# A four-layer kernel on one core: tile steps, group ends and tail of the first layer rearranged

## The reference, cut to what matters

```python
xBC = silu(causal_conv(xBC, conv_w))           # width 4, per channel
dt = softplus(dt_raw + dt_bias); a = dt * -exp(A_log)
cum = cumsum(a) within a chunk of 128 tokens
Yd   = (C B^T * exp(cum_i - cum_j) * dt_j, lower triangle) @ xs
S    = S * exp(cum_last) + states of the chunk;  Yoff = exp(cum) * C @ S_before
y = (Yd + Yoff + D * xs) * silu(z)
yn = y * rsqrt(mean(y * y) + eps) * norm_w;    x += yn @ W_out.T
...
x += shared expert + sum over the 2 chosen experts of share * (silu(g) * u) @ w_down[e]
```

```python
qkv = xn @ w_qkv.T + b;  out = softmax(q k^T / 16) v @ w_out.T
scale = max(mean(|w|), 1e-8);  w = clip(round(w / scale), -1, 1)   # for w1 and w2
```

## Time and profile before

| | |
|---|---|
| three runs | 1669.63, 1669.21, 1664.41 us; median 1669.21 |
| the profiled execution | 1666.6 us, span 1664.9 us, mean granted clock 0.895 |
| PE busy | 1332.4 us (80%), 7251 instructions |
| DVE, ACT, POOL busy | 914.0 (55%), 535.9 (32%), 409.2 (25%) |
| DMA | 88.83 MB, mean 53 GB/s |

### The profile page before, as it was taken

One profiled execution on the slowest core, in us unless ns is written; L12 is line 12 of the kernel. 1 busy time (PEld: TensorE's weight loads), 2 busy tenths in 40 slices (PEclk: granted clock), 3 DMA queues, 4 the chain that ended last, 5 costly groups with the idle time before them and its releaser, 6 DMA issues. The chain is left out here.

```text
span 1664.9 us, 21457 instructions
## 1 busy us (share of the span) xinstructions
PE 1332.4 (80%) x7251; PEld 823.5 (49%) x7251; DVE 914.0 (55%) x1888; ACT 535.9 (32%) x885; POOL 409.2 (25%) x380
## 2 busy tenths in 40 slices
PE   5556787779777675799999987998655599988987
PEld 3334544554455344457766744544343264644564
DVE  4755455536553766512211378988867435557434
ACT  1444336623752362221212222332302122233321
POOL 3267214512443365200040011000013500000035
PEclk9776999999999877899999988999855698999999
DMA  9122112210222122300000060000001200111113
GB/s 356 51 85 92 36 29 74 80 28 27 94 63 60 37 98 72 113 0 1 0 0 0 0 228 0 0 1 0 1 3 38 83 19 20 32 39 57 55 48 114
DMA packets 68240, 88.83 MB, mean 53 GB/s; under 512 B 15334, under 2 KB 51494, under 8 KB 67497
## 3 DMA queue, kind: packets, MB, share of 16 engines
q1 hardware_dynamic: 61996, 70.76, 12.9%
q0 software_dynamic: 6144, 16.79, 3.3%
HBM read 61.14 MB, written 26.38 MB: 53 GB/s over the span
## 5 line engine op out<-in xcount | busy, mean ns | idle before, releaser
L387 PE MATMUL l_banks<-l_xnT,all_region_a 128*128 128x512 f32 x288 | 131.5, 612 | 0.0
L1819 PE MATMUL l_banks<-l_xnT,mid_region_c 128*128 128x512 f32 (+1 forms) x192 | 96.2, 654 | 17.5 <-DVE l_xnT L2002 17.5
L853 POOL TENSOR_TENSOR all_region_b<-all_region_b,l_lc 128x512 f32<-128x512 f32 x64 | 84.8, 1344 | 83.2 <-DMA all_region_b<-l_lc_rows 83.1
L2662 POOL TENSOR_TENSOR l_rstd<-l_moments,all_neg_half 128x4 f32<-128x4 f32 x20 | 20.6, 1030 | 337.5 <-DVE l_moments L2702 337.5
L867 POOL TENSOR_TENSOR l_rw<-l_xdt,l_decay 128x512 f32<-128x512 f32 x64 | 69.9, 1120 | 76.0 <-DVE l_xdt L1104 76.0
L387 PEld LDWEIGHTS l_banks<-l_xnT,all_region_a 128*128 128x128 f32 x288 | 56.0, 197 | 65.2 <-issue 63.7
L387 PE MATMUL l_banks<-all_region_a,l_xa 128*128 x234 | 68.8, 414 | 20.6 <-issue 14.1
L1124 DVE TENSOR_TENSOR all_region_b<-all_region_b,l_cbd 128x512 f32<-128x512 f32 x64 | 65.7, 1028 | 19.4 <-ACT all_region_b L696 15.4
L1819 PEld LDWEIGHTS l_banks<-l_xnT,mid_region_c 128*128 128x128 f32 (+1 forms) x192 | 37.7, 202 | 68.3 <-issue 49.5
L696 ACT ACTIVATE all_region_b<-all_region_b 128x512 f32<-128x512 f32 x64 | 69.2, 1081 | 4.3
L1077 DVE SCALAR_TENSOR_TENSOR l_xbc<-l_pre,all_cols,l_xbc 128x512 f32<-128x512 f32 x72 | 61.6, 856 | 5.8 <-issue 0.4
(11 more groups left out here) (442 smaller groups left out, 2860.9 us busy)
## 6 DMA issues: line engine op xcount, KB each, us to landing
all_region_b<-l_lc_rows SPq DMA_DIRECT2D x64, 256.0 KB
l_xa<-slots_in SPq DMA_DIRECT2D x39, 128.0 KB, 3.2
slots_out<-l_xa SPq DMA_DIRECT2D x39, 128.0 KB, 3.3
mid_vector_rows<-slots_in SPq DMA_DIRECT2D x39, 128.0 KB, 2.1
slots_out<-all_region_a SPq DMA_DIRECT2D x39, 128.0 KB, 1.7
slots_in<-l_xp SPq DMA_DIRECT2D x4, 1024.0 KB, 12.7
all_region_a<-l_gate_up SPq DMA_DIRECT2D x1, 4096.0 KB, 14.4
all_x<-x SPq DMA_DIRECT2D x4, 512.0 KB, 6.0
```

The costliest lines, as they stand in the source:

```text
L387: return nc.tensor.matmul(out, lhsT, rhs, start=start, stop=stop, **kw)
L853: nc.gpsimd.tensor_tensor(bc[:, k, :, :], bc[:, k, :, :], spread(lc[:, c, heads], 1, BLK), ALU.subtract).then_inc(dd_ready.sem, 1)
L1819: return nc.tensor.matmul(out, lhsT, rhs, start=start, stop=stop)
L2662: nc.gpsimd.tensor_tensor(rstd[:, :], moments[:, :, 1], mem.neg_half[:, 0:GT], ALU.pow).then_inc(rstd_ready.sem, 1)
```

## The change

- Tile steps start at group 0's chunk 3; six of group 1's and 2's places are doubled in their stead. Within a step the order becomes transposes of f, gate/up of f-1, down of f-3, transpose of f-2, on PE and in the bank table; ACT copies the transposes first. The expert's number for the next gate/up product is read behind the present one (`owner_of`).
- `from_before` is cut: the far product (`within_chunk`) is made behind the first near product. DVE's `from_state` is cut too (`next_state`); in chunk 0 it stands before the first near product.
- Group ends: the first projection of the next group and the sums (now in banks 4 to 6) come before the last output product; DVE and ACT follow, with `out_stats` and `out_add` of the last chunk behind convolutions 0 and 1.
- Head: five of group 0's convolutions lie between the transposed copies of the head.
- POOL: all scatters of the first 8 tiles before group 0's differences, the other 8 tiles two at a time within chunks 0 and 1; all fetches have places of their own, 12 tiles are fetched before group 3's first weights; the adds lie four per chunk in group 3.
- Layer 1's folds, ternary weights, first statistics and first normalisation are done in layer 0's last group and behind it. Shared places in SBUF change so that these live on (`mem.xa`).

```diff
@@ places, bank order
-    places = [... if (g, c) >= (0, 2)]
-    places = sorted(places + [places[-1], places[-3]])
+    places = [... if (g, c) >= (0, 3)]
+    places = sorted(places + [places[4 * i + 6] for i in range(STEPS - len(places))])
-        back = (("gu", f - 1), ("th", f - 2), ("dn", f - 3), ("tx", f))
+        back = (("tx", f), ("gu", f - 1), ("dn", f - 3), ("th", f - 2))
+        names.insert(len(names) - (CONV_BLK + Z_BLK - 1 if g > 0 else 0), ("sums", g))
@@ PE
+        def owner_of(i):
+            if i < MOE_TILES:
+                expert[i] = pe.value_load(owner[0:1, i:i + 1], min_val=0, max_val=N_EXP - 1)
         def tile_step(f):
...
-                n = expert[i] = pe.value_load(owner[0:1, i:i + 1], min_val=0, max_val=N_EXP - 1)
...
                 jobs.fill(last, ("gu", i))
+                owner_of(i + 1)
...
         for g in range(GROUPS):
-            sums(g)
             if g > 0:
...
-                for j in range(CONV_BLK + Z_BLK):
+                in_proj(g, 0)
+            sums(g)
+            if g > 0:
+                out_proj(g - 1, NCH - 1)
+                for j in range(1, CONV_BLK + Z_BLK):
                     in_proj(g, j)
...
                     near(g, c, k)
+                    if k == 0:
+                        within_chunk(g, c)
...
+                if (g, c) == (GROUPS - 1, 2):
+                    pe.wait_ge(weight_sum, 1)
+                    jobs.wait_room(pe, 0, "weight_mean")
+                    jobs.fill(mm(jobs.bank("weight_mean")[:, 0:2], ones[:, :], wabs[:, :]), "weight_mean")
                 assemble(g, c)
-            out_proj(g, NCH - 1)
+        pe.wait_ge(l1.fold_sem, 16 * 2)
+        fold("w_qk", 0, l1.qkv[:, DK:2 * DK, :])
+        fold("w_vo", 2 * DK, l1.out)
+        out_proj(GROUPS - 1, NCH - 1)
+        fold_biases()
@@ ACT
+            if g > 0:
+                in_proj(g, 0)
+                square(g - 1, NCH - 1)
             block_sums(g)
...
+                if (g, c) == (GROUPS - 1, 1):
+                    act.wait_ge(l1.sem, 16 * 2)
+                    for i, part in enumerate((l1.w1, l1.w2)):
+                        last = nc.scalar.activation(below, part.rearrange("p a n -> p (a n)"), ACT.Abs,
+                                                    accum_out=wabs[:, i:i + 1])
+                        act.drain()
+                    act.drain().then_inc(weight_sum, 1)
@@ POOL
-            if t >= PAIRS:
-                pool.wait_ge(added.sem, added.done(0, t - PAIRS))
...
+        late = {0: ((8, 9), (10, 11)), 1: ((12, 13), (14, 15))}
+        for g in range(GROUPS):
+            if g == 0:
+                for t in range(2 * GT):
+                    scatter(t)
             if g == GROUPS - 1:
                 for t in range(2 * GT):
                     fetch(t)
             differences(g, 0)
+            if g == GROUPS - 1:
+                for t in range(2 * GT, 3 * GT):
+                    fetch(t)
             weigh(g, 0)
             for c in range(NCH):
+                ahead, behind = late.get(c, ((), ())) if g == 0 else ((), ())
                 if c + 1 < NCH:
                     differences(g, c + 1)
+                    for t in ahead:
+                        scatter(t)
                     weigh(g, c + 1)
                 if c > 0:
                     out_scale(g, c - 1)
                 gate(g, c)
+                for t in behind:
+                    scatter(t)
                 if g == GROUPS - 1:
-                    for t in range(2 * GT + 2 * c, 2 * GT + 2 * c + 2):
+                    for t in ((12, 13), (14,), (15,), ())[c]:
                         fetch(t)
@@ DVE
             turned("early", n, xnT2)
             if n > 1:
                 side(n - 1)
+            for j in range(2 * n - 2, min(2 * n, EARLY_CONVS)):
+                conv(0, j)
...
-            for j in range(CONV_BLK):
+            for j in range(EARLY_CONVS if g == 0 else 0, CONV_BLK):
                 conv(g, j)
-                if g == GROUPS - 1:
-                    add(j)
+                if g > 0 and j == 0:
+                    out_stats(g - 1, NCH - 1)
+                if g > 0 and j == 1:
+                    out_add(g - 1, NCH - 1)
...
+                if c == 0:
+                    from_state(g, c)
+                    near(g, c, 0)
+                else:
+                    near(g, c, 0)
                     take_y(g, c - 1)
-                from_state(g, c)
+                    from_state(g, c)
+                next_state(g, c)
                 near(g, c, 1)
...
+                if g == GROUPS - 1:
+                    add(4 * c + 0)
...
+                if (g, c) == (GROUPS - 1, 1):
+                    measure(0)
+                if (g, c) == (GROUPS - 1, 2):
+                    thresholds()
+                    quantise(0)
             take_y(g, NCH - 1)
             out_add(g, NCH - 2)
...
+        normalise(0, xn, 1)
+        take_folds()
+        quantise(1)
+        out_stats(GROUPS - 1, NCH - 1)
+        out_add(GROUPS - 1, NCH - 1)
+        take_biases()
```

269 lines of the change are left out of this document (127 added, 142 removed).

## The result

The changed kernel takes 1616.49 us, median of four runs (1615.80 to 1622.53), where the kernel before took 1669.29 beside it (four runs, 1664.41 to 1669.63): a ratio of 0.9698, 95% interval 0.9669 to 0.9728. The forecast was 1592 with a range from 1568 to 1628. The direction and the range hold; of a gain of 77.5 us in the span 51.0 came. (The profiled execution took 1615.8 us, its span is 1613.9.)

A forecast was written before the change was run, and what follows sets the result against it. No engine is full in layer 0, so a chain of waits through in-order engines bounds it; 23 + 10 + 4 + 10 + 9 + 15.5 - 2 + 8 = 77.5 us off 1666.6, plus 2.6 for the median, gives 1592, range 1568 to 1628.

The forecast's parts named there:

- rival 1: Tile steps: their idle comes back as waits for DVE or ACT, 29 us less gain, 1621 us; chance 0.20.
- I book a loss of 2: Last group's chunks: a loss of 2 us, bounded by a gain of 4 and a loss of 8.
- Chunks 0 and 1 have that room on DVE: Last group: DVE, 52.8 of 82.6 us busy, has room in these chunks for the additions and layer 1's work.
- ACT's wait for the late weights: Last group: ACT's absolute sums wait for w1 and w2, making the copy for chunk 2's assembly 5 us later.
- I take 0.85 a step: Groups 1 and 2: waits in each tile step shrink by 0.85 us, within bounds of 0 and 1.26.
- under 4 in group 1: Sign: PE's waits for the freeing of the gate/up bank fall from 11.9 us to under 4 there.
- wrong if near products are waited for in groups 1 and 2: Sign against the forecast: PE waiting for near products in these groups, where it never did before.
- the two halves, 0.61 and 0.66: Idle us in a tile step: 0.61 before the gate/up product (register load), 0.66 before the next tile's transposes (bank).
- The 2 us for the far product: Chunk 0: far product behind the first near product takes 2 us off in groups 1 and 2, 1 in group 3.
- An added step: Each tile step added to a group costs 2.3 us of work and 0.6 of bank waiting, 2.9.
- the rest, 14.4, as before: Group boundary: PE's work after nine projections and two units stays at 14.4 us, within a boundary of 45.3.
- Rival 3: DVE starved by POOL: all twelve pairs of differences and weights hold a product 9.0 us; 31 slower, 1700; chance 0.03.

The follow-up runs named there:

- e1: Changed kernel without the arithmetic of layer 0's 16 expert additions, the fetches kept; median 1595.21 us, last group's chunks 82.9 us.
- e8: Changed kernel with the last group's additions placed where DVE stood idle without them, fetches of tiles 8 to 11 behind the weights; median 1601.12 us, chunks 89.3.
- e11: Changed kernel, fetches behind the weights, additions 0/7/0/5/1/3 (before chunks, chunk ends, tail), absolute sums and first quantisation one chunk later; median 1598.56 us, chunks 84.2.
- e9: Changed kernel with the old order of a step's four jobs and the register load back before its gate/up product; median 1632.99 us.
- e5: Changed kernel with the old order of a tile step's four jobs and no early convolutions in the head; median 1650.88 us.
- e6: Changed kernel with the register load of the expert's number back in front of its gate/up product; median 1622.19 us.
- e7: Changed kernel with the far product back in front of the first near product; median 1617.23 us.
- e4: Changed kernel with the 16 additions where the kernel before had them, the fetches left as changed; median 1618.84 us, last group's chunks 86.7.
- e2: Changed kernel with thresholds and first quantisation moved from the last group's third chunk to the tail behind the folds; median 1617.04 us.
- e3: Changed kernel with the fetches of tiles 8 to 11 behind POOL's weights of the last group's first chunk; median 1617.47 us.
- e10: Changed kernel, fetches behind the weights, additions: seven at chunk 0's end, none in chunk 1, three, three, three in the tail; median 1603.17 us, chunks 89.4.
- e12: Changed kernel, additions 0/7/0/5/1/3, fetches ahead of the weights, absolute sums before chunk 2's square, quantisation before chunk 3's output-bank read; median 1600.62 us.

## Why the prediction was right and where it was not

The measured 1616.5 us lies in the range but outside the forecast's own range (1577 to 1608), and nearest to rival 1's 1621, though only a small part of the shortfall has rival 1's reason. That it fell inside the stated range is in part luck: one term missed its own bounds by 13 us (a loss of 21.2, bounded at 8), and the three boundaries gave 5.8 us back for a reason that I hadn't seen.

**The step that failed** is "I book a loss of 2" for the last group; 21.2 were lost. I had written "Chunks 0 and 1 have that room on DVE", from a busy time of 52.8 in 82.6 us. But room as a share of a stretch is not room between two near products that PE waits for. The kernel before had eight additions in that stretch, two ahead of the first near product and six at the ends of chunks, where DVE waits for PE; the change puts 16 there, in each chunk one in front of the third near product, one in front of the fourth and two behind it. e1 gives their price, 21.1 us; e8 and e11 show that 14.7 and 19.8 us come off the chunks with other places, in e11 with later sums too and with 2.6 of it back in the tail. The sum to make was four chunks with 4.4 us of additions each on the queue that PE waits for, 17.4, and the held instructions on top. What I had feared there, ACT's wait for the late weights, was 2.3 us.

**Chunks of groups 1 and 2** ("I take 0.85 a step"): the direction is right, the size is not. 0.53 and 0.32 a step came (e9). The idle time before the expert products went as promised. The bank wait didn't: my sign was a fall from 11.9 to "under 4 in group 1", and it is 5.0 before the transposes and 9.1 in all. I had given the bank one near product more of time, and at the doubled places there is none between two steps; the jobs behind the steps that want the same bank I had not looked at. Rival 1 holds for another part: near products are waited for, 7.0 and 7.1 us in the two groups, by my own sign ("wrong if near products are waited for in groups 1 and 2") a step gone wrong; but 3.8 of group 1's stand there in e9 too, so 3.2 are what the steps' idle came back as. I also added the two halves, 0.61 and 0.66; by e5, e6 and e9 the load ahead brings something only with the new order. The 2 us for the far product are nothing (e7). An added step was 2.6, not 2.9.

**Boundaries** gained 1.5 to 2.4 us more than written. The stretch rows tell why: the same 144 matmuls keep PE busy 47.6 us before and 43.1 after, at a granted clock of 0.91 and 1.00, that is part of the time at the lower of its two levels (1.2 of 2.4 GHz) before and all of it at the upper now. Of the 11.5 us at the first boundary 7.0 are idle time that went and 4.5 are this. I had copied "the rest, 14.4, as before", and it held slow rows, behind an idle time of 3.11 us that is 0.76 now:

```profile
212.74 1.97 PE L396 MATMUL l_banks<-all_region_a,l_hT 128*128 128x256 f32 x8 [0.76 <-DVEq L1162]
```

In the earlier trace rows these eight took 3.34. The reverse stands in the last group, where PE's busy time rose from 54.1 to 56.6 at a clock of 0.67 instead of 0.73. No run undoes the new order of the group ends or of the tail, so these gains rest on the two traces alone, but for the additions' part of the third (e4).

**Head and group 0**: the first chunk starts 17.4 earlier (14 forecast); e5 has 15.0 of it in the five convolutions. In the chunks POOL's steps came 4 to 5 us earlier than in my list (its weights of chunks 1 and 2 end at 116.99 and 137.98, 121.8 and 142.6 there), and then a near product of DVE was held for POOL's whole run:

```profile
145.25 9.72 DVE L1194 TENSOR_TENSOR all_region_b<-all_region_b,l_cbd 128x512 f32<-128x512 f32 x1
```

```profile
145.37 4.92 POOL L917 TENSOR_TENSOR all_region_b<-all_region_b,l_lc 128x512 f32<-128x512 f32 x4
150.26 4.16 POOL L931 TENSOR_TENSOR l_rw<-l_xdt,l_decay 128x512 f32<-128x512 f32 x4
```

PE stood 9.32 us for it. Assembly at 182.15, forecast 178.6. The same code has 93.7 to 96.0 us for this phase over the runs, so 1 or 2 us of any term in it mean nothing.

**Tail**: layer 1's transposes came right behind the block's end (633.52), 17.7 us behind the assembly, forecast 16. PE's biases end at 623.9, and 9.6 us go by from there; in e4, with two more additions on DVE, it is the same 9.62. It isn't PE's end that sets it, nor DVE's: in the changed kernel and in all twelve others that first transpose comes 5.97 us behind the end of DVE's last output addition (L1018 in the changed kernel), whatever DVE still does behind that. So additions behind it were free, and e2's quantisation ahead of it was not. What runs in the 5.97 us isn't shown.

**Rival 3** (DVE starved by POOL) was right in kind: five DVE instructions of the changed kernel's group 0 and last group take 4.3 to 9.7 us beside POOL. The kernel before has three (6.50, 5.04 and 9.71 us), not the one that I had counted. At one loss of 9.0 and four of 3.6 to 4.9 they are far from the twelve of 9.0 that its price counted. The Trainium skill (SBUF — State Buffer, section "SBUF: two separate sides") gives the pair to whoever starts first "for the whole instruction"; e8's addition and the near product above don't agree with one instruction, they came out behind the eighth. Nor does the start decide as the page has it: the near product's record begins 0.12 us ahead of POOL's first difference (145.25 and 145.37), chunk 1's addition 0.13 ahead, and both were held. Its other half, that on DVE's side it takes two SBUF inputs (or a faster mode), agrees: of the instructions that start beside a POOL product in the changed kernel, those that read a bank (L1200, L1215, L1221) all keep their 0.68 to 0.69 us, 18 of them, while the two-input ones (L1147, L1224, L1267) take 0.9 to 1.8 and the near products 0.7 to 5.2.

## What to carry to other kernels

Work that is moved onto a queue costs its full length if it stands between two results that the bounding engine waits for, however idle that queue is on the mean; look for the queue's own waits for the bounding engine and put it there, and measure again after each other change, since those waits move. Two idle times in one step that wait for the same chain are not added. Time moved from one stretch to the next is booked in both. And an operation that another engine's run can hold should not stand beside that run where the bounding engine waits behind it.

## What the runs showed that was not expected

- A two-input DVE instruction beside a run of POOL products was now and then held until the run was over, not for one instruction of it: 9.72 us (eight POOL instructions), about 8.5 of the 11.29 in e8 (eight), 5.0 of the 5.59 in e4 (four), where it takes 0.5 to 0.7 alone. Most others that began in such a run took 0.7 to 1.8. What decides between the two stays open; no run was made for it.
- The register load ahead of time (0.61 us of idle time gone) brought 2.9 and 4.5 us (groups 1 and 2) with the new order of the jobs, and nothing that could be seen with the old one.
- Layer 1's first transpose comes 5.97 us behind DVE's last output addition of layer 0 in thirteen kernels, also where DVE works on behind it (to 2.2 us ahead of the transpose in e8, 5.6 in the changed kernel).
- Eight indirect fetches issued by POOL and the broadcast rows loaded by SP slow each other when they run together: the fetches land after up to 6.6 us instead of 2.8, the last row is used 2.5 us later (e3), and chunk 0 of the last group takes 25.5 us instead of 20.4 (e10 against e12).
